# Image and text keys of the image-text attention in steps of their own, text keys of two contexts in one product

## The reference, cut to what matters

```python
ctx_img = context[:, :IMG_LEN]           # IMG_LEN = 257
ctx_txt = context[:, IMG_LEN:]           # 104 rows
q = rms_norm(linear(x, q_w, q_b), norm_q_w).reshape(B, L, NH, HD)
k = rms_norm(linear(ctx_txt, k_w, k_b), norm_k_w).reshape(B, -1, NH, HD)
...
k_img = rms_norm(linear(ctx_img, k_img_w, k_img_b), norm_k_img_w).reshape(B, -1, NH, HD)
...
img_x = attention(q, k_img, v_img)
txt_x = attention(q, k, v)
out = (txt_x + img_x).reshape(B, L, DIM)
return linear(out, o_w, o_b)
```

## Time and profile before

| | us |
|---|---|
| median of 3 runs | 2180.74 (2180.44 to 2181.41) |
| time of the profiled execution | 2178.68 |
| its span | 2176.9 |
| mean granted TensorE clock | 0.996 |
| PE busy / DVE busy / ACT busy | 2106.7 / 1502.5 / 1176.8 |
| this stage, from the first product to the barrier | about 1688 to 1811 |

### The profile page before, as it was taken

One profiled execution on the slowest core, in us unless ns is written; L12 is line 12 of the kernel. 1 busy time (PEld: TensorE's weight loads), 2 busy tenths in 40 slices (PEclk: granted clock), 3 DMA queues, 4 the chain that ended last, 5 costly groups with the idle time before them and its releaser, 6 DMA issues. The chain is left out here.

```text
span 2176.9 us, 35432 instructions
## 1 busy us (share of the span) xinstructions
PE 2106.7 (97%) x13214; PEld 1665.3 (76%) x13214; DVE 1502.5 (69%) x4042; ACT 1176.8 (54%) x3019; POOL 480.5 (22%) x444
## 2 busy tenths in 40 slices
PE   9998999999999999999998899999999999999998
PEld 6644888888888888888887797656656786665997
DVE  2396777777777877777666765676676757885555
ACT  2063767676766767676565444535534446773332
POOL 1210222212121212222111000243343010222442
PEclk9999999999999999999999999999999999999999
DMA  7013101111111101110100402133231330001300
GB/s 258 8 66 119 40 10 38 40 37 40 37 40 37 38 10 40 37 40 11 57 11 1 144 26 97 66 138 117 94 116 49 135 117 21 2 2 64 155 1 31
DMA packets 44179, 130.09 MB, mean 60 GB/s; under 512 B 6711, under 2 KB 21847, under 8 KB 40039
## 3 DMA queue, kind: packets, MB, share of 16 engines
q1 hardware_dynamic: 32488, 108.32, 13.8%
q10 hardware_dynamic: 9504, 8.50, 1.3%
q0 software_dynamic: 2016, 11.01, 1.3%
HBM read 108.05 MB, written 19.37 MB: 59 GB/s over the span
## 5 line engine op out<-in xcount | busy, mean ns | idle before, releaser
L821 PE MATMUL psum<-la_w_both,context 128*128 128x256 f32 (+1 forms) x1536 | 343.7, 380 | 1.4 <-DMA la_w_both<-in_qa_kv 1.4
L821 PEld LDWEIGHTS psum<-la_w_both,context 128*128 128x128 f32 (+1 forms) x1536 | 277.2, 184 | 46.5 <-DMA la_w_both<-in_qa_kv 1.7
L807 PE MATMUL psum<-qa_w,room 128*100 128x256 bf16 (+1 forms) x3072 | 265.7, 247 | 3.2 <-PEq L60 3.2
L807 PEld LDWEIGHTS psum<-qa_w,room 128*100 128x100 bf16 x3072 | 254.6, 125 | 4.1 <-issue 4.1
L931 ACT ACTIVATE qa_prob<-psum,qa_nm 100x361 f32<-100x361 f32 x128 | 71.9, 561 | 167.5 <-DVE qa_nm L1070 167.4
L1181 POOL TENSOR_TENSOR qa_w<-qa_w_raw,qa_w 128x768 bf16<-128x768 f32 x28 | 46.0, 1644 | 366.5 <-DVE qa_w L1012 366.5
L2724 ACT ACTIVATE it_prob<-psum,it_nm 100x257 f32<-100x257 f32 (+1 forms) x256 | 101.7, 412 | 38.6 <-DVE it_nm L2755 38.5
L1032 DVE BATCH_NORM_STATS2 qa_st<-psum 100x6 f32<-100x128 f32 x320 | 69.7, 285 | 75.1 <-PE psum L807 74.5
L1187 POOL TENSOR_TENSOR qa_o<-la_w_qt,qa_o 128x512 fp32r<-128x512 f32 x32 | 40.6, 1268 | 350.6 <-DVE qa_o L1020 350.6
L1061 DVE TENSOR_SCALAR qa_nrm_t<-psum,qa_mv,qa_sd 100x128 f32<-100x128 f32 x320 | 107.9, 404 | 2.4
L843 PE MATMUL psum<-qa_kxT,qa_qT 128*100 128x361 f32 x256 | 98.8, 468 | 1.3 <-ACT qa_qT L925 1.3
(11 more groups left out here) (374 smaller groups left out, 5119.7 us busy)
## 6 DMA issues: line engine op xcount, KB each, us to landing
qa_w_raw<-in_qa_w SPq DMA_DIRECT2D x8, 1536.0 KB, 6.5
la_gf_raw<-in_gf_w SPq DMA_DIRECT2D x16, 768.0 KB, 5.1
qa_piece<-in_tf_pieces ACTq DMA_DIRECT2D x64, 128.0 KB, 2.1
la_w_qt<-in_qa_o SPq DMA_DIRECT2D x8, 1024.0 KB, 5.3
context<-in_context SPq DMA_DIRECT2D x8, 722.0 KB, 11.9
gf_ternary<-la_gf_made POOLq DMA_DIRECT2D x7, 768.0 KB, 3.8
gf_ternary<-keep POOLq DMA_DIRECT2D x7, 768.0 KB, 3.6
tf_ring<-in_tf_w SPq DMA_DIRECT2D x10, 512.0 KB, 3.6
```

Source lines behind the costliest of these rows:

```text
L807: mm = pe.matmul(psum[0:T, 2 + at // 512, at % 512:at % 512 + width], xq[:, kind, k, b * T:(b + 1) * T], w3[:, s, part, k, at:at + width], ...
L821: mm = pe.matmul(psum[0:rows, i // 2, (i % 2) * 256:(i % 2) * 256 + 256], ctxT[:, k, b * TC + t0:b * TC + t0 + rows], kv_raw[:, s, k, :], ...
```

## The change

Image keys and text keys become steps of their own, 15 in all, listed in `steps`. The text keys of contexts 2 and 3, of 5 and 4, and of 6 and 7 are one step each: one product of 208 columns that reads two neighbouring slots of the ring and writes one bank; ACT writes it out in two activations. The groups remain, for the squares and sums, with contexts 5 and 4 exchanged: `whole` says behind which step a group is complete and squared, `sum_in_front` ahead of which block of which step its sum of squares stands, on PE and its root on ACT. The outputs of the first image step now stand on ACT ahead of the layer norm's two roots. The slots, and the steps behind which contexts 4 to 7 are loaded, are listed by hand (`SLOT`, `LOAD`, `load_behind`), in the order 4, 6, 5, 7. Each step reports with `kq_mm` for each block, and waits for the bank of the step before.

```diff
     groups = [("k", 0, 0, TC), ("k", 1, 0, TC), ("q", 0, 0, HALF), ("k", 2, 0, TC), ("k", 3, 0, TC), ("q", 1, 0, HALF)] + [
-        ("k", b, 0, TC) for b in range(4, B)]
+        ("k", b, 0, TC) for b in (5, 4, 6, 7)]
+    TXT = TC - IMG
+    steps = [("image", (0,)), ("text", (0,)), ("text", (1,)), ("image", (1,)), ("q", (0,)), ("text", (2, 3)), ("image", (2,)),
+             ("image", (3,)), ("q", (1,)), ("text", (5, 4)), ("image", (5,)), ("image", (4,)), ("text", (6, 7)), ("image", (6,)),
+             ("image", (7,))]
+    whole = {1: 0, 3: 1, 4: 2, 6: 3, 7: 4, 8: 5, 10: 6, 11: 7, 13: 8, 14: 9}
+    sum_in_front = {(3, 0): 0, (4, 2): 1, (5, 3): 2, (7, 3): 3, (8, 2): 4, (9, 3): 5, (11, 3): 6, (12, 3): 7, (14, 2): 8}
+    SLOT = {1: 2, 2: 0, 3: 1, 4: 2, 5: 1, 6: 0, 7: 1}
+    LOAD = {1: 1, 2: 1, 3: 1, 4: 2, 5: 2, 6: 2, 7: 3}
+    load_behind = {4: 3, 6: 6, 5: 7, 7: 10}
...
             def load_context(b):
-                if b > RING:
-                    sp.wait_ge(S_["kq_mm"], (ordinal(b - RING) + 1) * C)
-                sp.dma_start(ctxT[:, (b - 1) % RING, :, :], a["context"][b]).then_inc(c_in[(b - 1) % RING], 16)
+                if b in load_behind:
+                    sp.wait_ge(S_["kq_mm"], (load_behind[b] + 1) * C)
+                sp.dma_start(ctxT[:, SLOT[b], :, :], a["context"][b]).then_inc(c_in[SLOT[b]], 16)
...
             load_context(2)
+            load_context(3)
             for b in range(B):
-                if b + 3 < B:
-                    load_context(b + 3)
+                if b < len(load_behind):
+                    load_context(tuple(load_behind)[b])
...
+            def products(s, c):
+
+                kind, at = steps[s]
                 for k in range(C):
...
+                        x0, x1 = (0, IMG) if kind == "image" else (IMG, TC)
+                        if at == (0,):
+                            src = early.first_context[:, k, x0:x1]
+                        else:
+                            src = ctxT[:, SLOT[at[0]]:SLOT[at[0]] + len(at), k, x0:x1]
+                    out = psum[:, (s * C + c) % 4, 0:wide(s)]
+                    if len(at) == 2:
+                        out = out.rearrange("p (b t) -> p b t", b=2)
+                    mm = pe.matmul(out, w[("q", "image", "text").index(kind)][:, k, c * P:(c + 1) * P], src,
                                    start=(k == 0), stop=(k == C - 1))
-                return mm
+                mm.then_inc(S_["kq_mm"], 1)
...
                 for c in range(C):
-                    q = n * C + c
-                    if c == 2:
-                        square_sum(n - 1)
-                    pe.wait_ge(S_["kq_out"], q - 3)
-                    for segment in segments(g):
-                        mm = products(g, c, q, segment)
-                    mm.then_inc(S_["kq_mm"], 1)
-            pe.wait_ge(S_["kq_out"], len(groups) * C)
+                    if (n, c) in sum_in_front:
+                        square_sum(sum_in_front[n, c])
+                    pe.wait_ge(S_["kq_out"], n * C + c - 3)
+                    products(n, c)
+            pe.wait_ge(S_["kq_out"], len(steps) * C)
...
+            def out(n, c):
+
+                kind, at = steps[n]
+                act.wait_ge(S_["kq_mm"], n * C + c + 1)
+                bank = psum[:, (n * C + c) % 4]
+                for i, b in enumerate(at):
...
+                    last = act.activation(to, src, ACT.Identity, bias=core.param(bias, c))
+                last.then_inc(S_["kq_out"], 1)
+
+            for c in range(C):
+                out(0, c)
             for h in range(2):
                 act.wait_ge(S_["var_ready"], h + 1)
...
+                elif n in whole:
+                    g = groups[whole[n]]
+                    if whole[n]:
+                        act.wait_ge(S_["ssq_mm"], whole[n])
+                    act.activation(sq[:, :, 0:width(g)], place(g), ACT.Square).then_inc(S_["sq_ready"], 1)
             root(len(groups) - 1)
```

More of the change, by code:

```diff
@@ L2352, in width, with wide @@
             return g[3] - g[2]
+        def wide(s):
+            kind, at = steps[s]
+            return HALF if kind == "q" else IMG if kind == "image" else TXT * len(at)
         def place(g):
@@ L2361, in segments @@
             return [(0, IMG, 1, "k_img_b", "nki_w"), (IMG, TC, 2, "k_b", "nk_w")]
-        def ordinal(b):
-            return groups.index(("k", b, 0, TC))
         @block.sync
@@ L2397, in variance @@
                     S_["var_ready"], 1)
-            def products(g, c, q, segment):
-                x0, x1, wi, _, _ = segment
+            def products(s, c):
+                kind, at = steps[s]
                 for k in range(C):
-                    if g[0] == "q":
-                        src = X[:, k, g[1] * HALF + g[2]:g[1] * HALF + g[3]]
-                    else:
-                        src = ctxT[:, (g[1] - 1) % RING, k, x0:x1] if g[1] else early.first_context[:, k, x0:x1]
-                    mm = pe.matmul(psum[:, q % 4, x0:x1], w[wi][:, k, c * P:(c + 1) * P], src,
+                    if kind == "q":
+                        src = X[:, k, half_of(at[0])]
+                    else:
+                        x0, x1 = (0, IMG) if kind == "image" else (IMG, TC)
[7 more added lines that the diff above has]
+                    mm = pe.matmul(out, w[("q", "image", "text").index(kind)][:, k, c * P:(c + 1) * P], src,
                                    start=(k == 0), stop=(k == C - 1))
-                return mm
+                mm.then_inc(S_["kq_mm"], 1)
             def square_sum(n):
@@ L2418, in _ @@
             pe.wait_ge(last.context_in, 16)
-            image, text = segments(groups[0])
             for c in range(C):
-                products(groups[0], c, c, image)
+                products(0, c)
                 if c < 2:
@@ L2426, in _ @@
             pe.wait_ge(S_["w_kt"], 16)
-            for c in range(C):
-                products(groups[0], c, c, text).then_inc(S_["kq_mm"], 1)
-            for n, g in enumerate(groups):
+            for n, (kind, at) in enumerate(steps):
                 if n == 0:
                     continue
-                if g[0] == "k":
-                    pe.wait_ge(c_in[(g[1] - 1) % RING], 16 * ((g[1] - 1) // RING + 1))
-                else:
+                if kind == "q":
                     pe.wait_ge(S_["w_q"], 16)
-                    pe.wait_ge(S_["ln_normed"], 2 * g[1] + 2)
+                    pe.wait_ge(S_["ln_normed"], 2 * at[0] + 2)
+                elif at != (0,):
+                    for b in at:
+                        pe.wait_ge(c_in[SLOT[b]], 16 * LOAD[b])
                 for c in range(C):
-                    q = n * C + c
-                    if c == 2:
-                        square_sum(n - 1)
-                    pe.wait_ge(S_["kq_out"], q - 3)
-                    for segment in segments(g):
-                        mm = products(g, c, q, segment)
-                    mm.then_inc(S_["kq_mm"], 1)
-            pe.wait_ge(S_["kq_out"], len(groups) * C)
+                    if (n, c) in sum_in_front:
[3 more added lines that the diff above has]
+            pe.wait_ge(S_["kq_out"], len(steps) * C)
             pe.wait_ge(S_["normed"], groups.index(("q", 0, 0, HALF)) + 1)
@@ L2463, in _ @@
                 act.activation(qn[:, :, quarter_of(q)], Y[:, :, quarter_of(q)], ACT.Square).then_inc(S_["ln_sq_ready"], 1)
+            def out(n, c):
[3 more added lines that the diff above has]
+                for i, b in enumerate(at):
+                    if kind == "q":
+                        to, src, bias = qn[:, c, half_of(b)], bank[:, 0:HALF], "q_b"
+                    elif kind == "image":
+                        to, src, bias = kT[:, c, b, 0:IMG], bank[:, 0:IMG], "k_img_b"
+                    else:
+                        to, src, bias = kT[:, c, b, IMG:TC], bank[:, i * TXT:(i + 1) * TXT], "k_b"
+                    last = act.activation(to, src, ACT.Identity, bias=core.param(bias, c))
+                last.then_inc(S_["kq_out"], 1)
+            for c in range(C):
+                out(0, c)
             for h in range(2):
@@ L2467, in _ @@
                     S_["std_ready"], 1)
-            for n, g in enumerate(groups):
+            for n in range(1, len(steps)):
+                final = n + 1 == len(steps)
                 for c in range(C):
[L2470 to L2477, removed]
+                    if (n, c) in sum_in_front:
+                        root(sum_in_front[n, c])
+                    out(n, c)
+                    if final and c == 2:
+                        g = groups[-1]
                         act.wait_ge(S_["kq_out"], n * C + 3)
-                        act.wait_ge(S_["ssq_mm"], n)
                         act.activation(sq[:, 0:3, 0:width(g)], place(g)[:, 0:3], ACT.Square).then_inc(S_["sq_ready"], 1)
                 act.wait_ge(S_["kq_out"], (n + 1) * C)
-                if n + 1 == len(groups):
+                if final:
```

(2 more changed lines are left out.)

## The result

The changed kernel takes **2184.85 us** in the median of nine runs (2181.73 to 2189.56), before it is 2180.75 in runs taken beside it: a ratio of **1.0020, interval 1.0011 to 1.0028**. Eleven more runs, under the name again, gave 2182.45 (2180.89 to 2188.82), ratio 1.0014 (1.0005 to 1.0023). By the ratios it is 3 to 4 us slower (the two pairs of medians stand 4.1 and 1.8 apart), next to the 0.2% that bounded "the same". The forecast was 2183.4, range 2178.6 to 2186.5. The stage's first product starts at 1687.26 where it started at 1688.15; "rel" is a time from there.

A forecast was written before the change was run, and what follows sets the result against it. PE, 97% busy, paces the stage, but its end waits for DVE. PE's terms came to -0.1 and had no part; tail +1.8 and clock +0.9 gave +2.7 on 2180.74: 2183.4 us, range 2178.6 to 2186.5.

The forecast's parts named there:

- Pair product, -3.9: Text keys of contexts 2 to 7: one 208-column product per pair at 0.178 us a record saves 3.9 us of PE time.
- Rivals 2 and 4: Text pair product: 2, it costs as two, 2186.4, 12 in 100; 4, as cheap as one narrow, 2181.4, 3 in 100.
- First sum, +1.9: First sum of squares moves forward: PE stands 2.8 us for DVE where it stood 0.87, costing 1.9 us.
- The walk: Step-by-step timing of the new order on PE, sums against ACT and DVE chains; products end at 1806.2, before 1806.0.
- S2: Predicted start on PE of group 2's sum of squares, 1733.9; S with another number is that group's sum.
- The waits: PE's added stalls for DVE's additions or the chain before sums 4, 7 and 8: 0.2, 1.3 and 0.4 us.
- The tail, +1.8: Stage's end: last sum waits for DVE, 8.14 us behind sum 8, so it starts at 1810.1, 1.8 us later.
- The clock, +0.9: Idle PE before first sum and at the tail may bring half clock; half of one 1.7 us stretch, 0.9 us.
- Loads: Seven context loads, landing in 4.1 to 10.7 us, arrive before they are wanted: cost nothing.

The follow-up runs named there:

- Last_apart: Changed kernel with the last text pair split (text 6, image 6, text 7, image 7) and sum 8 ahead of image 7; 2178.27 us, ratio 0.9997.
- best_pairs_apart: Changed kernel with last text pair split, first sum two blocks later, and remaining pairs made as two 104-column products each; 2178.30 us, ratio 0.9992.
- no_idle: Changed kernel with first sum two blocks later and three idle products on PE before the last sum; 2179.04 us, ratio 0.9991.

## Why the prediction was right, and where it was off

**Pair product, -3.9.** Right in size: 0.176 us a record against 0.178 taken from the line through two other widths. The reason that I gave for the line was wrong, though: 208 columns do not lie between two widths that lie on it. They lie below both, 257 and 400, and above 104, which is off the line. So this was an extrapolation, and it came out. Rivals 2 and 4 (nothing, or everything) are excluded by that row. The rule of the Trainium skill ("TensorE: Matmul & The Clock Gate", The mechanism), that loads don't overlap products on the same rows of the array, would have made a pair chunk cheaper by a whole load per record, an estimate of 0.9 us a chunk by that page's figure for a load (LDWEIGHTS). The measured saving is 0.33, and the trace does not agree with the rule.

**First sum, +1.9.** Right: 2.64 us of wait against 2.8, where 0.87 was. The 2.8 went from start to start and the 0.87 did not; by one measure the term is +1.8. Group 1 was complete at rel 28.30 before (1716.45 in rows 2) and is now at 30.06, so +1.8, with no pair product made yet. Removing the wait brought 2.9: from start to start it is 2.8 long (the list of waits counts the end of the last product as busy), and the product behind a sum that PE did not wait for starts 0.1 sooner.

**The walk.** The sums stand where it put them, in rel, predicted and measured: S2 45.8 and 45.6, S4 68.2 and 67.8, S6 92.9 and 92.3, S7 100.8 and 100.2, S8 113.8 and 113.0. It ran late by a little at each pair (1.41, not 1.43) and in the chain behind an image step, shorter by 0.2 as the text allowed. The waits: 0.2, 1.3, 0.4 predicted; 1.20 is the only one of the later three that the list of PE's waits shows. From start to start the one before sum 4 is 0.2 (two query chunks from 1749.45 end at 1754.85, the sum starts at 1755.05).

**The tail, +1.8.** The mechanism is right (8.22 us behind sum 8, 8.14 predicted), the term is +1.1, since sum 8 stood at rel 113.0 and not at 113.8. Last_apart shows that it is the place of sum 8 and not PE's work that set the end.

**The clock, +0.9.** This is the term that was mis-sized. I named both places and priced one stretch at up to 1.7 us, and took half of one. A stretch behind the barrier measured 3.0 (8.62 against 5.61), one behind the first sum 3.0 as well (10.6 against 7.6), since both lasted about twice as long as the one of rows 8; others lost 1.7 (last_apart behind the first sum, best_pairs_apart behind the barrier). That the barrier's own 1.8 us of idle brings none was read from one execution; with a last wait of only 0.31 half clock followed it in two of three. The median moves between 2182.5 and 2184.9 from one set to the next, and the interval reaches to both sides of 0.2%. That the two idle times cause part of it is supported by the table of the profiled executions and by no_idle. That they cause most of it is not shown: best_pairs_apart has neither and spreads as wide, and the profiles have half clock in untouched code as well, ahead of the stage and behind it. Which runs without a profile had which stretch was not seen.

**The sum.** Forecast +2.7, by the medians measured +4.1 in one set and +1.8 in the other. The tail was taken 0.7 too dear and the clock, in the first set, some 2.1 too cheap; that the total came out so near is in part luck.

**Loads** cost nothing: no wait of PE for a context appears.

What the change was worth is then: -3.9 from the product, given back in its new order by a wait ahead of sum 0, one ahead of sum 7, a tail that hangs on DVE, and some 0.7 to 3 us (what the two medians leave over the 1.1 of the stage), which I put down to the clock without having seen it run by run.

## What to carry to other kernels

When products are cut or merged, walk every wait behind them again: here the merged product saved what its arithmetic says, and all of it was lost because sums of squares were placed where DVE was not ready, and the last but one too late. At the end of a stage, count back from the last engine's chain, not from the busiest engine's work; giving up 1.4 us of PE time brought the end of the stage 1.8 us forward. And count a new idle time of PE at more than its length: here waits of 2.45 and 2.64 us were at times followed by another 3 us lost to the clock. Before calling that the cause of a spread, look at the clock in the rest of the kernel too.

## What the runs showed of the hardware

A wait of 2.64 us on a PE that was busy on both sides was followed by half the clock in one profiled execution (again) and by none in another (after), the same instructions in the same order; with the kernels that keep this wait it was three of five. In again the granted clock stood at 0.52 over the 6.3 us behind it, and the work there took 3.0 us longer, more than the wait itself.

Untouched code, too, has half clock in some executions and not in others: the window from 1190 to 1206 is at 0.79 in four of the ten profiles and at 1.00 in six.

In a chunk of 104-column records behind an image chunk a record takes 0.109 us, and in two such chunks in a row 0.111 (1.78 us for sixteen); 208 columns take 0.176, though the product reads two slots of the ring that lie 1444 elements apart and writes them into one bank.
